# First half of the final sums moved between the results of routed tiles 28 to 38, their gate weights into the shared stage

## The reference

```python
x = x + tanh(g_xattn[0]) * attention(layernorm(x), ctx, ctx, mask, ...)
xf = layernorm(x).reshape(-1, D)
shared = mean over s of (gelu(xf @ sW1[s] + sb1[s]) @ sW2[s] + sb2[s])
gates = xf @ rW + rb
topk_vals, topk_idx = top_k(gates, 2)
topk_probs = softmax(topk_vals)                    # two weights for each token
moe = sum over the 2 chosen e of topk_prob * (gelu(xf @ W1[e] + b1[e]) @ W2[e] + b2[e])
x = x + tanh(g_ffn[0]) * (shared + moe)
```

## Time and profile before

| what | value |
|---|---|
| median of 3 runs | 455.94 us (453.99 to 456.85) |
| the profiled execution | 454.94 us, span 453.1 us |
| mean granted TensorE clock | 0.977 |
| PE busy | 386.3 us (85%) |
| DVE busy | 384.9 us (85%) |
| ACT busy | 340.8 us (75%) |
| POOL busy | 309.7 us (68%) |

### The profile page before, as it was taken

The page is one execution under the profiler, slowest core; times in us unless marked ns, Lnnn a source line. Parts: engine busy times, 40 slices in busy tenths (PEclk is TensorE's granted clock), DMA queues, the critical chain, the costliest instruction groups (busy, mean ns, idle before and its releaser), DMA issues.

```text
span 453.1 us, 14622 instructions
## 1 busy us (share of the span) xinstructions
PE 386.3 (85%) x5155; PEld 316.6 (70%) x5155; DVE 384.9 (85%) x947; ACT 340.8 (75%) x677; POOL 309.7 (68%) x431
## 2 busy tenths in 40 slices
PE   0558889997999899988789999998999999999910
PEld 0335677786788788766557776777899999999900
DVE  7696668978876987899778999887799999999986
ACT  0635677787888788878789986775888888888844
POOL 6252222799899899978777767774177777777740
PEclk9999999999999999999899999999999999999975
DMA  7968884354333334474221111112223333355229
GB/s 192 314 196 214 206 186 110 90 138 98 92 92 98 87 95 107 101 229 175 92 66 49 55 37 53 49 48 69 70 83 96 97 90 93 94 156 158 69 78 294
DMA packets 71686, 53.43 MB, mean 118 GB/s; under 512 B 7209, under 2 KB 63476, under 8 KB 71616
## 3 DMA queue, kind: packets, MB, share of 16 engines
q1 hardware_dynamic: 64896, 43.15, 35.9%
q0 software_dynamic: 4544, 8.44, 5.6%
q10 hardware_dynamic: 2176, 0.91, 0.8%
HBM read 29.51 MB, written 24.33 MB: 119 GB/s over the span
## 4 chain that ended last, share of the span: by engine, by line
POOL 23%; PE 21%; DVE 20%; issue 13%; DMA 10%; SPq 6%; ACT 4%; POOLq 0%; DVEq 0%; ACTq 0%
POOL yd L650 9%; DVE HH L1533 5%; PE pAtt L1144 4%; DMA scr<-QKS 4%; PE pAtt L1090 2%; PE pS L1132 2%; PE pE L1132 2%; DVE t_MX L1257 2%; POOL t_STG L558 2%; POOL t_W2l L562 2%; POOL QKS L548 2%; PE pAtt L928 1%; DMA t_STG<-in_W 1%; POOL xs L628 1%; POOL t_XF L572 1%
## 5 line engine op out<-in xcount | busy, mean ns | idle before, releaser
L650 POOL DMA_INDIRECT yd<-Y,XR x78 | 86.8, 1113 | 37.6 <-issue 23.2
L1257 DVE TENSOR_REDUCE t_MX<-pS 128x4 f32<-128x512 f32 x128 | 86.8, 682 | 22.6 <-PE pS L889 20.0
L748 ACT ACTIVATE PT<-pE,t_mbias,t_scl 128x512 f32<-128x512 f32 x128 | 96.9, 789 | 2.7 <-PE pE L889 2.7
L628 POOL DMA_INDIRECT xs<-t_STG,t_pos x64 | 66.2, 1034 | 23.1 <-issue 14.3
L1563 DVE SCALAR_TENSOR_TENSOR HR<-GG,t_sc,HR 128x512 f16<-128x512 f32 x78 | 58.6, 751 | 2.8
L1144 PE MATMUL pAtt<-t_W2h,HR 128*128 x624 | 59.2, 219 | 0.7 <-DVE HR L1563 0.7
L889 PE MATMUL pS<-t_K,t_Q 128*128 128x128 f16 x512 | 52.0, 228 | 8.5 <-DVE t_MX L1257 5.1
L1144 PE MATMUL pAtt<-t_W2l,HR 128*128 x312 | 54.4, 219 | 0.0
L828 ACT ACTIVATE GG<-pS,t_b1T,t_inv 128x256 f32<-128x256 f32 x78 | 39.8, 561 | 16.9 <-PE pS L1132 16.9
L889 PE MATMUL pE<-t_Q,t_K 128*128 128x128 f16 x512 | 49.9, 220 | 1.6 <-DMA t_Q<-MPl 0.6
L1144 PEld LDWEIGHTS pAtt<-t_W2h,HR 128*128 128x128 f16 x624 | 49.6, 98 | 1.1 <-issue 0.9
(11 more groups left out here) (280 smaller groups left out, 1042.7 us busy)
## 6 DMA issues: line engine op xcount, KB each, us to landing
xs<-t_padrow SPq DMA_DIRECT2D x10, 516.0 KB, 5.1
XR<-xs SPq DMA_DIRECT2D x39, 129.0 KB, 2.3
scr<-QKS SPq DMA_DIRECT2D x16, 256.0 KB, 2.4
t_Q<-scr SPq DMA_DIRECT2D x16, 256.0 KB
t_K<-scr SPq DMA_DIRECT2D x32, 128.0 KB
t_STG<-in_W SPq DMA_DIRECT2D x7, 512.0 KB, 6.6
YY<-yd SPq DMA_DIRECT2D x14, 256.0 KB, 4.2
t_X<-in_x SPq DMA_DIRECT2D x4, 512.0 KB, 7.7
```

Of the source, the lines that this page charges most:

```text
L628: g.indirect_dma_start(k.xs, bass.IndirectOffsetOnAxis(ap=pos[:, n:n + 1], axis=0), k.PAY[:, n, :], None).then_inc(h.di[q], 16)
L650: g.indirect_dma_start(k.yd, bass.IndirectOffsetOnAxis(ap=XR[u][:, q, D:ROW], axis=0), Y[u][:, q, :], None, bounds_check=2 * T - 1, oob_is ...
L748: act.activation(PT[:, m % NPT], pE[g % 2][:], ACT.Exp, bias=k.mbias[:, bt:bt + 1], scale=k.scl[:, bt:bt + 1]).then_inc(s.exp, 1)
L1257: v.tensor_reduce(out=MX[:, n // G % 2, n % G // 4, m % 2, m // 2::2], in_=pS[n % 2][:], axis=AX_X, op=ALU.max).then_inc(s.max, 1)
```

## The change

- **Weights.** ACT takes tanh(d/2) in unit 11 of the shared stage (`GATED`), in place of exp behind the last tile. DVE makes `w1` and `w2` of it in unit 13 in four small instructions, two on a column of halves of the gate and two on 32 columns.
- **Sums of units 0 to 3.** On DVE they are cut in halves. From tile 28 on (`SUMMED`) a half stands behind each Y(i): two line 1585 instructions behind an even tile, and two more with the closing addition behind an odd one. The eight halves stand behind Y(28) to Y(35), and nothing is left for tiles 36 to 38. ACT's products of units 0 to 3 are cut in the same way, two instructions behind the copy of tile i + 3, for i = 28 to 35.
- **Sums of units 4 to 7** stay behind the last tile.
- **Stores.** SP has four stores, not two, ahead of its wait for all scatters, and four behind the loads.

```diff
-    STORED = 2
+    STORED = NQ // 2
+    SUMMED = FIRST_DONE + 5
...
+                    if i == GATED and c == 1:
+                        act.wait_ge(l.route, DIFFER)
+                        act.activation(ex[:], ix[:], ACT.Tanh, scale=0.5).then_inc(h.tanh, 1)
...
+            def weigh(n, part=range(R)):
+
+                if part[0] == 0:
+                    act.wait_ge(f.ld[1][n], 16)
+                for j in (R * n + r for r in part):
+                    ins = act.activation(YY[:, 1, j, :], YY[:, 1, j, :], ACT.Copy, scale=k.w2[:, j:j + 1])
+                if part[-1] == R - 1:
+                    ins.then_inc(f.w, 1)
...
-            act.wait_ge(l.route, DIFFER)
-            act.activation(ex[:], ix[:], ACT.Exp).then_inc(h.exp, 1)
...
+                if 0 <= i - SUMMED < NQ:
+                    n, half = divmod(i - SUMMED, 2)
+                    weigh(n, range(R // 2 * half, R // 2 * half + R // 2))
+            all_scattered(act)
+            for ahead in range(NQ // 2, NQ // 2 + AHEAD):
+                load_results(act, 0, ahead)
+            for n in range(NQ // 2, NQ):
+                weigh(n)
...
+                    if i == GATED + 2:
+                        next(gate_rows, None)
...
+            def sums(n):
+
+                rows = slice(R * n, R * n + R)
+                v.wait_ge(f.ld[0][n], 16)
+                for j in range(R * n, R * n + R):
+                    ins = v.scalar_tensor_tensor(out=k.X[:, j, :], in0=YY[:, 0, j, :], scalar=k.w1[:, j:j + 1], in1=k.X[:, j, :],
+                                                 op0=ALU.mult, op1=ALU.add)
+                    if j == R * n + R // 2 - 1:
+                        yield
+                ins.then_inc(f.x1, 1)
+                v.wait_ge(f.x1, n + 1)
+                v.wait_ge(f.w, n + 1)
+                v.tensor_tensor(k.X[:, rows, :], k.X[:, rows, :], YY[:, 1, rows, :], ALU.add).then_inc(f.sum, 1)
+                yield
...
                 routed_result(i, es[i])
-            weights_of_choices()
...
+                if i >= SUMMED:
+                    next(first_sums, None)
+            for _ in first_sums:
+                pass
+            for n in range(NQ // 2, NQ):
+                for _ in sums(n):
+                    pass
```

More of the change, by code:

```diff
@@ L3 @@
 from contextlib import ExitStack
-from itertools import accumulate
+from itertools import accumulate, chain
 F32 = mybir.dt.float32
@@ L41 @@
 PREFIX_UNIT = 4
+GATED = 11
 LAST_CHOICE = 8
@@ L319, in layer @@
     l = Parts(**{n: sem("l_" + n) for n in "rstd xf pay T XT G gate idx route count slots".split()})
-    h = Parts(**{n: sem("s_" + n) for n in "up gelu hi hia lo dn x exp wt".split()})
+    h = Parts(**{n: sem("s_" + n) for n in "up gelu hi hia lo dn x tanh wt".split()})
     FIRST, SECOND, DIFFER = 1, 4, 5
@@ L828, in routed_gelu @@
                 act.activation(G32[i % 2][:, c, :], pU[c][:, 0:TILE], ACT.Gelu, bias=k.b1T[:, bass.ds(e * NC + c, 1)], scale=k.inv[:, 3:4]).then_inc(r.gelu, 1)
+            def weigh(n, part=range(R)):
[5 more added lines that the diff above has]
+                    ins.then_inc(f.w, 1)
             es = tile_experts.of
+            act.wait_ge(h.wt, 1)
             act.wait_ge(h.lo, NC * (SUNITS - 1))
@@ L1412, in weights_of_choices @@
             def weights_of_choices():
[L1414 to L1418, removed]
+                v.wait_ge(h.tanh, 1)
+                v.tensor_scalar(k.halves[:, 0:1], k.gt[:, 1:2], 0.5, None, ALU.mult)
+                link(v.tensor_scalar(k.halves[:, 1:2], k.gt[:, 1:2], -0.5, None, ALU.mult))
+                yield
+                v.tensor_scalar(k.w1[:], ex[:], k.halves[:, 1:2], k.halves[:, 0:1], ALU.mult, ALU.add)
+                link(v.tensor_scalar(k.w2[:], ex[:], k.halves[:, 0:1], k.halves[:, 0:1], ALU.mult, ALU.add))
+                settle(v, h.wt)
+                yield
             def columns():
@@ L1458, in second_part @@
                 yield from tiles_of_experts()
-            first, second, last_rows, bias_rows = first_part(), second_part(), last_payload(), output_bias()
+            first, second, last_rows, bias_rows, gate_rows = first_part(), second_part(), last_payload(), output_bias(), weights_of_choices()
             def body(t, a, b, c, o):
@@ L1572, in routed_result @@
                                        op0=ALU.mult, op1=ALU.add).then_inc(r.y, 1)
+            def sums(n):
[5 more added lines that the diff above has]
+                    if j == R * n + R // 2 - 1:
+                        yield
+                ins.then_inc(f.x1, 1)
+                v.wait_ge(f.x1, n + 1)
+                v.wait_ge(f.w, n + 1)
+                v.tensor_tensor(k.X[:, rows, :], k.X[:, rows, :], YY[:, 1, rows, :], ALU.add).then_inc(f.sum, 1)
+                yield
+            first_sums = chain.from_iterable(sums(n) for n in range(NQ // 2))
             es = tile_experts.of
@@ L1611, in program @@
               identf=([P, P], F32), ident16=([P, P], F16), ones=([P, P], F32), onesb=([P, P], BF16), lower=([P, P], BF16),
-              b2=([P, E * D], F32), b1T=([P, NE * NC], F32), gt=([P, 2], F32), outc=([P, 1], F32), padrow=([P, PAD * ROW], I32), rb=([P, E], F32),
+              b2=([P, E * D], F32), b1T=([P, NE * NC], F32), gt=([P, 2], F32), outc=([P, 1], F32), halves=([P, 2], F32), padrow=([P, PAD * ROW], I32), rb=([P, E], F32),
               rW=([P, 2 * E], F16), sc=([P, 6], F32), inv=([P, 6], F32), bound=([P, 6], F32), pow2=([P, 6], F32), down=([P, 2], F32), mv=([P, NT, 2], F32),
```

## The result

The changed kernel takes 460.52 us (median of 4 runs, 459.99 to 461.37), the kernel before 455.21 us (4 runs, 453.99 to 456.85). The ratio is 1.0116, with a 95% interval of 1.0077 to 1.0155: slower by 1.2%. The profiled execution took 459.99 us with a span of 457.8 us, 4.7 us more than the span before.

The account below looks back on a forecast made before the run. PE set the 2.87 us a tile with DVE only 0.11 us behind; POOL was late behind the last tile. 454.94 + 6.2 (loop) - 0.4 (tail) = 460.7 us, or 461.7 from the median; predicted 461.2, range 458.2 to 464.2.

Parts of the forecast that it names:

- two starting points: Start of the sum: the profiled execution gave 460.7 us, the median of three runs 461.7; the middle, 461.2, was predicted.
- Sums on DVE: Tiles 28 to 35: four units of 1.78 us against 0.11 us slack a tile put Y(37) 6.2 us later, bounds 5.5 to 7.0.
- POOL behind it: Behind Y(37): POOL's last four scatters, so the last scatter too, move with Y(37), 6.2 us later.
- ACT, waits in the loop, weights: Loop and shared stage: each costed at 0; ACT's products 1.2 us if tiles stayed at 2.87, weights at most 0.5.
- The tail: Behind the last scatter: stores moved into the loop gain 0.4 us, between 0 and 0.9, by earlier scatter landing and faster loads.
- PE's gaps: Tiles 28 to 35: PE waits about 0.8 us for DVE in each tile, at 3.65 us a tile on DVE.
- third rival: Loop: scatters and sums shut each other out, 0.6 us for each of eight halves, 4.8 us in all, 465.5 us; chance 0.05.
- The sums did not fit in beside PE: First rival, in the loop: hidden DVE waiting absorbs part of the 7.12 us, delay under 2 us, about 456 us; chance 0.07.
- the clock stayed at 1.00: Fifth rival, tiles 28 to 35: PE's clock falls in its new gaps, 17 us more, 478 us; chance 0.02.
- second rival: Tail's DMA queues: two fewer stores gain 2 us plus 0.4 on the scatter, sums nearly free, 452.5 us; chance 0.05.
- fourth rival: Tile 28: unit 0's second load comes 2 us late, DVE stands still about 1.2 us, about 462.4 us; chance 0.05.
- lower bound with 1.64 us a unit: Sums in the loop: only 1.14 us of four instructions and about half a microsecond of the fifth count, delay 5.5 us.

## Why the prediction was right

The time (461.2 forecast, 460.52 measured, range 458.2 to 464.2) and the sign came out, and the steps can be checked one by one. The number is closer than its terms, which is in part luck: the sum gave a rise of 5.8 us where the spans differ by 4.7. The loop came out 0.15 over, the tail 0.7 under, and Y(28) happened to start 0.55 earlier; and the 461.2 was the middle between two starting points.

1. *Sums on DVE.* Y(37) was to come 6.2 us later, from nine tiles of 2.76 and four units of 1.78; it came 6.35 later. The 0.15 lies in the four tiles with three sums, which took 4.05 us each where 2.76 + 1.25 = 4.01. The step that carried the forecast was to take DVE's pace not from its busy share (29.08 of 30.00 beside PE's 29.60) but from one tile in which it had fallen behind the earlier trace rows. With 0, 2 and 4 units in the loop, and with the four doubled, the stretch took 25.75, 28.46, 32.10 and 38.69 us, which is shown by runs, not argued.
2. *POOL behind it* moved with Y(37), to the hundredth (5.21 us both times).
3. *ACT, waits in the loop, weights* were costed at nothing and cost nothing that the times show: 0.26 us in the stretch for ACT's products alone, none for the weights, and no wait for a load. Where DVE's tiles stay at 2.87, ACT's products were priced at 1.2 us, which was too much. The first load on DVE's way was given a microsecond of room; in the trace after it had some 2.3 (issued at 399.44, landed 3.3 us later, wanted at 405.05).
4. *The tail.* I took -0.4, between 0 and -0.9; it was -1.10 (the last four rows of the table that are not zero). The term that was mis-sized is the last scatter's landing, 0.4 at most by the median of all scatters: it gained 0.97. The median stands for scatters within the loop. What was in flight while the last scatter was under way (queue, kind: packets, MB, share of 16 engines; q0 is the scatter itself, q1 loads and stores) was in the kernel before

```profile
q1 hardware_dynamic: 972, 0.49, 54.2%
q0 software_dynamic: 64, 0.00, 1.5%
q14 instruction: 1, 0.01, 0.6%
```

in the kernel before without early stores

```profile
q0 software_dynamic: 64, 0.00, 1.8%
q14 instruction: 1, 0.01, 0.8%
```

and in the changed kernel

```profile
q0 software_dynamic: 64, 0.00, 2.2%
```

This sorts all nine kernels. The five that landed at 2.14 or 2.15 us had nothing else in flight, the two at 2.64 had store packets (q1) alone, the one at 2.73 had one packet of the instruction queue (q14) alone, and the kernel before, at 3.12, had both. So a part of the 0.97 goes with the stores of units 0 and 1, as I said, and a part with a packet that I hadn't looked for. That each of the two delays the landing is likely and not settled: the stores were taken away in two kernels, but the instruction packet was not under my control. That the stores of units 2 and 3 are worth little, as I said, is borne out by the kernel with two early stores.

5. *PE's gaps* were to be 0.8 us a tile, 6.2 in the stretch. PE's matmul rows show about 0.2 in a tile with two sums and 0.7 in one with three, 4.2 in all; the rows of the weight loads for the same matmuls show 6.3 (total, times, longest):

```profile
PEld pAtt L1155 <- issue: 6.3, 13, 1.0
PE pAtt L1155 <- DVE HR L1579: 4.2, 12, 0.8
```

The ends of matmul rows are modelled, and the same 355 matmuls count as 27.91 us where they were 25.26. So the 4.2 is likely too small, which is not shown.

The third rival, scatters and sums that shut each other out, would have given 465.5 us. It didn't come: a unit took 1.78 us in the loop as behind it. One of its signs did, scatters longer than 1.22 us. POOL in the changed kernel, and the split beside the second of these scatters:

```profile
409.20 1.33 POOL L652 DMA_INDIRECT yd<-Y,XR  x1 [0.92 <-DVE Y L1587]
...
435.25 1.27 POOL L652 DMA_INDIRECT yd<-Y,XR  x1 [1.43 <-DVE Y L1587]
```

```profile
435.58 0.48 DVE L1577 TENSOR_SCALAR HR<-GG,t_sc 128x512 f16<-128x512 f32 x1
```

The first ran beside a sum and the split at 409.59, the second beside a split with no sum near, so the stretching needs no sum. POOL had waited for `Y` before both, so it cost nothing. The Trainium skill, "SBUF — State Buffer", section "Who interferes with whom", states its rule on VectorE instructions with two SBUF inputs for GpSimd instructions that read SBUF, and not for ones that only write it. No run here shows which of the two a scatter is; the 1.78 us, read behind the last tile while scatters ran, say that the rule did not act on these sums.

The other rivals were settled by the runs as well. The sums did not fit in beside PE (2.71 and 6.35 us for two and four units), no instruction waited for a load, and the clock stayed at 1.00 through the stretch. The second rival's sign was met, for the tail from the last scatter's start is 457.8 - 441.97 = 15.83 us, 1.10 under 16.9; but it gives back 1.10 of 6.35, so it doesn't decide.

Some of the prediction's sums were off by a little, without weight for the result. The fourth rival's wait is 404.6 + 2 - 405.6 = 1.0 us, not 1.2. The lower bound with 1.64 us a unit is 5.65, not 5.5. The range's lower end by its own rule is 453.99 + 4.6 = 458.6, not 458.2. And its chances add up to 0.75 for slower and 0.01 for faster, not 0.74 and 0.02.

## What to carry to other kernels

Work that stands in the shadow of a wait is free; before it is moved into a loop, compare the room there with its cost on the same engine. Where two engines are both nearly full, busy shares don't say which has room: look for a stretch in which one of them had fallen behind, and read its step without waits. Here DVE had 0.11 us a tile, and the rest of the 7.12 us showed up in the time one for one, less about a microsecond that the tail gained.

## What the runs showed of the hardware

With the sums doubled, PE had gaps of 1.4 to 1.6 us in every second tile, and the granted clock fell once in the stretch. Busy time by stretch of that kernel:

```profile
424.00:428.00 4.00, 2.66 (x34) 2.42 (x35) 3.89 (x11) 1.90 (x5) 1.32 (x2) 1.00 0.72 223
...
432.00:436.00 4.00, 2.20 (x31) 1.85 (x29) 3.93 (x10) 2.43 (x6) 1.26 (x2) 0.97 0.34 102
436.00:440.00 4.00, 4.00 (x35) 3.20 (x33) 3.93 (x10) 2.26 (x4) 2.12 (x2) 0.60 0.10 35
440.00:444.00 4.00, 2.60 (x32) 2.04 (x29) 3.89 (x9) 1.94 (x4) 2.15 (x2) 1.00 0.27 75
```

The columns behind PE's busy time are as above; the clock is the third from the right. After 2.20 busy of 4.00 us it fell to 0.60 on average, most of the way to its lower level (1.2 GHz is 0.50), for one tile, and PE needed all of 4.00 us for it; after 2.66 of 4.00 it stayed at 1.00. DVE's steps did not change, so the time did not show it. In the changed kernel, with gaps of up to 0.8 us, the clock was 1.00 over the whole stretch.

The tanh stood between gelus on ACT without a table load; exp, which it replaces, had one of 1.28 us in the kernel before. Of ACT in the kernel before, and in the changed one:

```profile
429.36 1.28 ACT L842 ACT_TABLE_LOAD   x1
```

```profile
289.87 0.22 ACT L814 ACTIVATE t_ex<-t_ix 128x32 f32<-128x32 f32 x1
```
